# A hand-scheduled attention and FP4 feed-forward kernel: its setup, with other operands on VectorE and part of the normalisation on GpSimd

## The reference

```
xn  = (x - mean) / sqrt(var + 1e-5)
q, k, v = split(xn @ w_attn + b_attn)          # 16 heads of 8
s   = q @ k.T * 8**-0.5 + mask                 # later keys only: -log(distance + 1), earlier keys: -inf
att = softmax(s) @ v @ w_proj + b_proj
h   = silu(fq(xn) @ fq(w_gate).T) * (fq(xn) @ fq(w_up).T)       # 352 wide
ffn = fq(h) @ fq(w_down).T
fq(z): blocks of 16 along the last dimension, scale = max|z| / 6, each value rounded to the FP4 grid
```

## Time and profile before

| | before |
|---|---|
| median of three runs | 626.64 us |
| the profiled execution, its own time | 626.35 us |
| its span in the profile | 624.5 us |
| TensorE busy | 564.4 us, 90% |
| VectorE busy | 562.8 us, 90% |
| GpSimd busy | 537.4 us, 86% |
| ScalarE busy | 400.8 us, 64% |

### The profile page before, as it was taken

The page is one execution under the profiler, slowest core; times in us unless marked ns, Lnnn a source line. Parts: engine busy times, 40 slices in busy tenths (PEclk is TensorE's granted clock), DMA queues, the critical chain, the costliest instruction groups (busy, mean ns, idle before and its releaser), DMA issues.

```text
span 624.5 us, 11270 instructions
## 1 busy us (share of the span) xinstructions
PE 564.4 (90%) x3807; PEld 250.9 (40%) x3807; DVE 562.8 (90%) x1178; ACT 400.8 (64%) x857; POOL 537.4 (86%) x400
## 2 busy tenths in 40 slices
PE   6999779999999999999989899999989898989985
PEld 5576534444343334333333332342334242432322
DVE  6899998989999999999999999998989999997661
ACT  4576457566656475767667577666656667759782
POOL 7226987789899989999998999999998999998992
PEclk9999988999999999999999999999999999999997
DMA  5255341310000000200000000000000000000000
GB/s 148 74 137 114 119 83 51 78 43 36 2 2 3 0 2 10 86 1 2 2 0 2 19 1 1 2 2 1 1 2 1 19 0 2 1 2 1 1 2 17
DMA packets 14715, 16.66 MB, mean 27 GB/s; under 512 B 1594, under 2 KB 14171, under 8 KB 14243
## 3 DMA queue, kind: packets, MB, share of 16 engines
q1 hardware_dynamic: 14123, 15.70, 9.2%
q10 hardware_dynamic: 536, 0.26, 0.2%
HBM read 11.75 MB, written 4.01 MB: 25 GB/s over the span
## 4 chain that ended last, share of the span: by engine, by line
PE 43%; POOL 32%; DVE 13%; ACT 7%; issue 4%; ACTq 0%; POOLq 0%; DVEq 0%
POOL ring L802 25%; PE psum L1396 11%; PE psum L1354 9%; PE psum L1378 7%; DVE mxp L1135 7%; ACT ring L954 2%; POOL xw L820 2%; POOL xw L818 2%; PE psum L1331 2%; POOL xw L822 2%; PE psum L1312 2%; PE psum L1314 1%; PE psum L1320 1%; DVE ring L1162 1%; PE psum L1404 1%
## 5 line engine op out<-in xcount | busy, mean ns | idle before, releaser
L802 POOL TENSOR_TENSOR ring<-ring,dist 128x1024 f32<-128x1024 f32 (+3 forms) x223 | 438.4, 1996 | 31.7 <-ACT ring L954 31.3
L1135 DVE TENSOR_REDUCE mxp<-psum 128x1 f32<-128x512 f32 (+3 forms) x640 | 352.6, 598 | 20.5 <-PE psum L1354 11.4
L954 ACT ACTIVATE ring<-psum 128x512 f32<-128x512 f32 (+3 forms) x446 | 211.5, 528 | 101.5 <-PE psum L1381 51.9
L1354 PE MATMUL psum<-kop,qop 96*128 96x512 bf16 (+3 forms) x640 | 198.0, 352 | 7.3 <-DVE mxp L1135 5.3
L1378 PE MATMUL psum<-qop,kop 128*128 128x512 bf16 (+3 forms) x640 | 190.7, 349 | 6.2 <-DVE mxp L1135 3.7
L1396 PE MATMUL psum<-ring,vaug 128*32 128x512 f32 (+3 forms) x1280 | 151.5, 544 | 15.0 <-POOL ring L802 14.1
L1162 DVE TENSOR_TENSOR ring<-psum,dist 128x512 f32<-128x512 f32 (+3 forms) x194 | 115.7, 622 | 13.9 <-ACT psum L954 13.8
L954 ACT ACTIVATE psum<-psum 128x512 f32<-128x512 f32 (+3 forms) x194 | 99.5, 543 | 39.7 <-PE psum L1378 23.4
L1354 PEld LDWEIGHTS psum<-kop,qop 96*128 96x128 bf16 x640 | 57.2, 97 | 127.8 <-DVE mxp L1135 46.5
L1378 PEld LDWEIGHTS psum<-qop,kop 128*128 128x128 bf16 x640 | 59.7, 97 | 82.2 <-DVE mxp L1135 15.5
L1357 PE MATMUL psum<-tri_q,identb 128*128 128x128 bf16 x256 | 56.2, 221 | 0.0
(11 more groups left out here) (130 smaller groups left out, 490.2 us busy)
## 6 DMA issues: line engine op xcount, KB each, us to landing
kop<-parts_dram SPq DMA_DIRECT2D x9, 384.0 KB
qop<-parts_dram SPq DMA_DIRECT2D x9, 384.0 KB
parts_dram<-qpart SPq DMA_DIRECT2D x18, 128.0 KB, 2.8
xin<-_attn_hidden_states_dram SPq DMA_DIRECT2D x4, 256.0 KB, 4.7
ring<-inv_dram SPq DMA_DIRECT2D x1, 1024.0 KB, 4.9
out_dram<-xin SPq DMA_DIRECT2D x4, 256.0 KB, 2.3
parts_dram<-qpart SPq DMA_DIRECT2D x6, 96.0 KB
qop<-parts_dram SPq DMA_DIRECT2D x3, 192.0 KB
```

Of the source, the lines that this page charges most:

```text
L802: g_.tensor_tensor(slot(p)[:, :, 0:n], slot(p)[:, :, 0:n], both, ALU.mult).then_inc(weighed_pool, 1)
L954: a_.activation(scores if pair_vec[p] else slot(p)[:, e % 2, 0:n], scores, ACT.Exp, scale=SCALE).then_inc(exp_done, 1)
L1135: v_.tensor_reduce(mxp[:, u % 2, 4 * a + j, c - g:c - g + 1], bank(*o)[:, 0:n], AX_X, ALU.max).then_inc(max_used, 1)
L1354: ins = mm(bank(*o)[:, 0:n], qop[0:K_MAX, u // NQ % 2, h, P * a:P * (a + 1)], kop[0:K_MAX, h, k0:k0 + n], start=True, stop=(c != g))
```

## The change

- **Normalisation.** VectorE still normalises chunk ci = 0. For the other three it works out mean and reciprocal deviation once for all 12 tiles, and GpSimd does the two elementwise steps (subtract, multiply) for each chunk, 128x512 each, as item `scale`.
- **First split.** The remainder of the bf16 split of chunk 0 stays in the PSUM bank of `qk` instead of going to the SBUF buffer `qc`; the bank is free only after the last step of the split.
- **Quantisation.** The reciprocals of the block scales and the exponent bits are written to a PSUM bank (`c4`), which each piece holds from stage 2 to stage 5; the scales lie in rows of 35 columns, written as 5 x 7. The weights are three pieces (384, 384, 352) instead of two of 560, and come after the four of `xn`. The wait for GpSimd moves from stage 4 to stage 5. Seven pieces in all.
- **Loads.** For the second group q and k come in two parts, heads 0 to 3 first (`next_loaded`), then the rest; the loads of the FFN weights move behind them in SyncE's queue, and GpSimd's memset that they wait for moves to the end of its constants.
- **ScalarE's constants** for later chunks are written in quarters (four instructions of 1024 columns).
- **Plan.** 20 instead of 30 warming transposes; ranks of `dist` and `v` go from 4 and 3 to 8, those of `sel` for heads 1 to 3 to 4.3; the max pass of unit 0 goes head by head; `CHUNK_AT` holds back `qk` and `v` and no longer the normalisation; an idle engine now steps to the nearest clock of any other engine.

```diff
-    add("DVE", ("inv",), 700, 100, [], rank=0)
-    add("DVE", ("kfill", 0), 3300, 100, [], rank=0)
+    add("DVE", ("inv",), 2150, 100, [], rank=0)
+    add("DVE", ("kfill", 0), 1750, 100, [], rank=0)
...
-        add("DVE", ("scale", ci), 2000, 100, [("ACT", ("sqrt", 0 if ci == 0 else NG - 1))], at=at, rank=1 if ci < 2 else 3)
-        pe(("xnT", ci), 8 * P, [("DVE", ("scale", ci))], rank=1)
+        if ci < 2:
+            add("DVE", ("scale", ci), (2800, 800)[ci], 100, [("ACT", ("sqrt", NG - 1 if ci else 0))], rank=1)
+        if ci:
+            pool(("scale", ci), 2600, [("DVE", ("scale", 1))], rank=2)
+        pe(("xnT", ci), 8 * P, [("POOL" if ci else "DVE", ("scale", ci))], rank=1)
...
-            pe(("sel", t, h), PARTS * GQ, [("DVE", ("rest", t, 1)), ("POOL", ("consts",))], rank=1)
+            pe(("sel", t, h), PARTS * GQ, [("DVE", ("rest", t, 1)), ("POOL", ("consts",))], rank=SEL_RANK if h else 1)
...
+            if kind == "fp4" and item[2] == 2 and len(free_banks(now)) < HELD_FREE:
+                return None
...
+        if engine == "DVE" and kind == "scale":
+            now = max(now, clock["POOL"] if pool_busy[0] else 0)
...
-            others = [clock[e] for e in busy if clock[e] > now]
+            if engine == "POOL":
+                pool_busy[0] = False
+            others = [clock[e] for e in busy if e != engine]
...
+                if o[0] == "scale":
+                    ci = o[1]
+                    tiles = slice(TPG * CHUNKS[ci], TPG * (CHUNKS[ci] + 1))
+                    xn = xw[:, 0:S].rearrange("p (t d) -> p t d", d=D)[:, tiles]
+                    pool.wait_ge(rstd_ready, 1)
+                    g_.tensor_tensor(xn, xin[:, tiles], moments[:, tiles, 0:1].to_broadcast([P, TPG, D]),
+                                     ALU.subtract).then_inc(centred, 1)
+                    pool.wait_ge(centred, ci)
+                    g_.tensor_tensor(xn, xn, st1[:, 0, tiles].rearrange("p (t o) -> p t o", o=1).to_broadcast(
+                        [P, TPG, D]), ALU.mult).then_inc(xn_pool, 1)
...
-                    ins = v_.tensor_scalar(sc[:, of], amax[:, of], 1.0 / 6.0, 1e-12, ALU.mult, ALU.max)
+                    ins = v_.tensor_scalar(sc[:, n].rearrange("p (a b) -> p a b", b=7), amax[:, n],
+                                           1.0 / 6.0, 1e-12, ALU.mult, ALU.max)
...
-                    ins = v_.reciprocal(amax[:, of], sc[:, of])
+                    bank_free_for(vec, "c4", n)
+                    ins = v_.reciprocal(bank("c4", n)[:, 0:nb], sc[:, n, 0:nb])
...
-                    if n:
-                        vec.wait_ge(fp4_seq, 2 * n)
-                    ins = v_.tensor_scalar(c.bitcast(I32), v.bitcast(I32), EXPONENT, None, ALU.bitwise_and)
+                    ins = v_.tensor_scalar(bank("c4", n)[:, 0:w].bitcast(I32), v.bitcast(I32), EXPONENT, None,
+                                           ALU.bitwise_and)
...
-                    v_.tensor_scalar(c, c, 1.0, ROUND, ALU.max, ALU.mult).then_inc(round_ready, 1)
+                    if n:
+                        vec.wait_ge(fp4_seq, 2 * n)
+                    v_.tensor_scalar(c, bank("c4", n)[:, 0:w], 1.0, ROUND, ALU.max, ALU.mult).then_inc(round_ready, 1)
...
-                        v_.scalar_tensor_tensor(out=rest(t), in0=bank("qk", 0, t), scalar=bqk[:, t:t + 1],
+                        v_.scalar_tensor_tensor(out=bank("qk", 0, t), in0=bank("qk", 0, t), scalar=bqk[:, t:t + 1],
...
-                        v_.tensor_tensor(qpart[:, t, 2], rest(t), qpart[:, t, 1], ALU.subtract).then_inc(part3_vec, 1)
+                        v_.tensor_tensor(qpart[:, t, 2], bank("qk", 0, t), qpart[:, t, 1],
+                                         ALU.subtract).then_inc(part3_vec, 1)
```

More of the change, by code:

```diff
@@ L131, in plan @@
             act(("p2", ci, t), GQ, [("DVE", ("rest", t, 0)) if ci == 0 else ("POOL", ("split", 2 * ci + t, 0))], rank=1)
-        pe(("v", ci), 4 * GQ, [("ACT", ("xnT", ci))] + first, rank=3)
+        pe(("v", ci), 4 * GQ, [("ACT", ("xnT", ci))] + first, at=at, rank=V_RANK)
         act(("v", ci), P, [("PE", ("v", ci))], n=4, rank=3)
         if ci:
-            add("ACT", ("kfill", ci), 3500, 200, first, at=at, rank=4)
-            if ci == 1:
-                add("ACT", ("qzero", 1), 3500, 200, first, at=at, rank=4)
+            for part in range(4):
+                if ci == 1:
+                    add("ACT", ("qzero", 1, part), 920, 200, first, at=at, rank=4)
+            for part in range(4):
+                add("ACT", ("kfill", ci, part), 920, 200, first, at=at, rank=4)
     for k in range(FILL):
@@ L145, in plan @@
     for k in range(NG):
-        pe(("dist", k), 4 * GQ, [("DMA", ("hankel",)), ("POOL", ("consts",))] + first, rank=4)
+        pe(("dist", k), 4 * GQ, [("DMA", ("hankel",)), ("POOL", ("consts",))] + first, rank=DIST_RANK)
         act(("dist", k), GQ, [("PE", ("dist", k))], rank=3)
@@ L176, in plan @@
                         needs = [("DMA", ("q", u // NQ)), ("DMA", ("k", CHUNKS.index(c)))]
+                        if u == NQ:
+                            needs = [("DMA", ("next", 0))]
                     if u >= 2:
@@ L251, in plan @@
     clock = {e: 800.0 for e in queues}
-    seen = {("DMA", ("x", ci)): 4700 + 700 * ci for ci in range(NG)}
+    seen = {("DMA", ("x", ci)): 4750 + 700 * ci for ci in range(NG)}
     seen[("DMA", ("hankel",))] = 25000
-    seen[("DMA", ("weights",))] = 52000
+    seen[("DMA", ("weights",))] = WEIGHTS_AT
     pair_vec, weighed_by = {}, {}
@@ L270, in released @@
               "up": ("ACT", ("gu",) + o[1:])}.get(kind)
+        if kind == "c4":
+            by = ("DVE", ("fp4", o[1], FP4_STAGES - 1))
         if kind == "sel":
@@ L273, in released @@
         if kind == "qk":
-            by = ("DVE", ("rest", o[2], 0)) if o[1] == 0 else ("ACT", ("qf",) + o[1:])
+            by = ("DVE", ("rest", o[2], 1)) if o[1] == 0 else ("ACT", ("qf",) + o[1:])
         if kind == "st":
@@ L332, in take @@
             issued[kind] += 1
+        if engine == "DVE" and kind == "fp4" and item[2] == 2:
+            o = ("c4", item[1])
+            b = min(free_banks(now), key=lambda k: (released(holder[k]) if holder[k] else 0, k))
+            bank_of[o], prior[o], holder[b] = b, holder[b], o
         if engine == "ACT" and kind == "st":
@@ L375, in take @@
                 seen[("DMA", ("k", ci))] = end + DMA_CHUNK
+                if ci == 1:
+                    seen[("DMA", ("next", 0))] = end + DMA_NEXT
                 for gi in range(1, NG):
```

208 lines of the change are left out of this document (120 added, 88 removed).

## The result

The changed kernel took 622.65 us, the median of five runs (622.03 to 623.89), against 626.68 us for the kernel before. The ratio is 0.9929, with a 95% interval of 0.9916 to 0.9941: faster by 0.7%, 4 us, where 12 us were forecast. The direction was right, the size was a third, inside the range from 605 to 624 only at its end. The profiled execution took 622.93 us, with a span of 621.2.

A forecast was written before the change was run, and what follows sets the result against it. VectorE was taken to bound the setup, sharing the steady stage's weighing with GpSimd. Terms of 12.3 + 2.4 + 1.8 = 16.5 us of VectorE's time, worth 10.4 to 16.5, were taken as 12: 614.5 against 626.64 us, range 605 to 624.

The forecast's parts named there:

- the part on the loads: SyncE's queue: weight loads moved behind the q and k loads cost nothing, covered by the four `xn` pieces going first.
- The port: VectorE's quantisation: product L1049 saves 2.8 us, exponent steps L1054 and L1058 1.7; PSUM operands cost 2.0 and 1.1.
- L1045: VectorE's scale in the quantisation: 3.1 us saved, with no instruction over about 0.2 us afterwards.
- L1080: Last step of the first split, before the first scores: 0.68 us each with one PSUM input, 1.4 us saved.
- The normalisation: VectorE's L1022: of 6.8 us, 1.84 stay for the first chunk and 5.0 us go.
- The head of the chain: TensorE's first transposes: fewer warming ones and the repaired idle rule start the chain 2.4 us earlier, near 10.3 us.
- The square root's 1.8 us: VectorE's idle wait near 31 us for ScalarE's root goes, by later `dist` and `v` and quartered constants: 1.8 us.
- The first weighing: GpSimd's first weighing, at 60.52 us before, was to start between 50 and 57 us.
- The rate of 0.63: Steady stage, weighing shared with GpSimd: 1 us of VectorE replaces 0.63 us of time, so 16.5 us give 10.4.
- The gain is given back: Rival: GpSimd is the real bound, VectorE's freed time turns idle; 624 us or no change, chance 0.13.
- Everything shifts: Rival: setup bound by VectorE alone, steady stage starts 16.5 us earlier; 610 us, down to 605, chance 0.25.
- The ping-pong through the shared buffer: Rival: stage 5 waits for GpSimd's step of the piece before, 3.7 us for six pieces; 636 us, chance 0.09.

The follow-up runs named there:

- experiment 1: Changed kernel with the plan told that the weights land at 78 us instead of 62 (`WEIGHTS_AT`), orders replanned: 613.50 us, ratio 0.9774.
- experiment 2: Changed kernel with the eight weight loads back in their old place in SyncE's queue, all orders unchanged: 612.46 us, ratio 0.9770.
- experiment 4: Changed kernel with the weight loads early and the quantisation through SBUF instead of the PSUM bank: 619.14 us, ratio 0.9880.
- 11: Changed kernel with early weight loads and the remainder of the first split in its SBUF buffer again, orders unchanged: 613.71 us, ratio 0.9777.
- 7: Changed kernel with early weight loads and the last three chunks' normalisation back on VectorE, replanned: 611.90 us, ratio 0.9752.
- 6: Kernel before with only the new idle rule and 20 instead of 30 warming transposes: 624.91 us, ratio 0.9954.
- experiment 12: Changed kernel with early weight loads, the second group's q and k loaded whole, and the plan told when they land: 612.74 us, ratio 0.9774.
- Experiment 9: Changed kernel with early weight loads, the last three chunks' normalisation on VectorE and 100 instead of 200 fillers: 617.35 us, ratio 0.9838.
- experiment 10: Changed kernel with early weight loads and the second group's q and k loaded whole, orders unchanged: 628.22 us, ratio 1.0009.

## Why the prediction was wrong

**The step that failed** is this one of the part on the loads: "I cost the move at nothing: the cover is the four pieces of `xn` that go ahead." The cover ran out at 67.7 us, the weights landed at about 75.7. I looked at what the queue move took away from the stores and not at when the moved loads would arrive. The plan's own number for it, raised with the move from 52 to 62 us, was not checked against the queue. The queue of the kernel before:

```profile
24.37 2.20 SPq L640 DMA_DIRECT2D qop<-parts_dram  x3
...
30.12 1.31 SPq L633 DMA_DIRECT2D kop<-parts_dram  x3
...
31.94 7.17 SPq L690 DMA_DIRECT2D xw<-in_L_ffn_w_gate_dram  x1
...
40.60 1.50 SPq L692 DMA_DIRECT2D wp<-in_L_attn_w_proj_dram  x1
```

From the first of its twelve loads to the issue of the last weight load it takes 16.2 us, with one slow issue of 7.17 us among them, and that load lands 6.6 us later. Counted from 45.84 us, where the changed kernel's twelve loads start, this gives a landing at 68.7 us (an estimate). It would have shown that there was no margin, and that 62 us was wrong, but only 1 us of the wait: the changed kernel has two slow stretches in its queue, 7.07 and 7.42 us, where the kernel before has one.

The move cost a wait of 8.0 us, and 9 to 10 us of time (experiments 1 and 2). What the lower clock had in the 1 to 2 us beyond the wait was not measured by itself. The last sign that the prediction named for being wrong, that VectorE's idle time near the pieces grows, is what came. Without the wait the kernel takes 612.5 or 613.5 us, where 614.5 were forecast.

**The other steps.**
- The port, that is, what VectorE loses to GpSimd in the product and the exponent steps. In the sum, the product and the two steps of the exponent gave 4.5 us less 3.1 us for PSUM, a net of 1.4. The runs give 6.7 us for the same operands (4 against 2). The durations were right, but the stretches would have been longer in the new order: 1330 ns for the product instead of the 1012 of the earlier trace rows. The new order fills GpSimd earlier (7.42 against 0.64 us from 30 to 40 us), so that more of these steps have a GpSimd instruction beside them.
- L1045. I expected nothing over 0.2 us. Its successor L1144 took 1.04, 0.67 and 0.76 us; against the 3.1 us taken, the group's 3.6 us for seven instructions hold 3.6 - 7 x 0.18 = 2.3 us of stretch still, so that 0.8 us went. Without the wait for the weights, in experiment 2, the seven take 4.5 us, and nothing went. This term should have been near zero.
- L1080: 1.4 us was the right size for the wrong reason. The stretch is gone in SBUF too (11); the order took it away, not PSUM.
- The normalisation: 5.0 us of VectorE's time taken as gain. Given back to VectorE they are 3.25 us and cost no time (7). The term was too high by 1.75 us in its size, and no run shows that the rest reaches the end.
- The head of the chain, 2.4 us: transposes at 10.00 us instead of 10.3. The two lines alone gave 2.4 us, but with the shorter wait for the square root in it (6).
- The square root's 1.8 us: in the changed kernel VectorE has no wait of its kind left, and maxima run in its place. Its share of the time was not measured.
- The first weighing was to start between 50 and 57 us. It starts at 59.76, against 60.52 before. But GpSimd's idle time in front of it did shrink: it is busy for 39.3 of the first 60 us in experiment 2 and for 25.6 before, since the normalisation (6.2 us) and much of the quantisation and splitting moved in there. The memset of `hT`, which follows its last step of the last piece, comes 13.2 us earlier in experiment 2, the second row here, than in the kernel before:

```profile
107.90 0.31 POOL L793 MEMSET hT<- 1x256 f32 x1
```
```profile
94.71 0.31 POOL L884 MEMSET hT<- 1x256 f32 x1
```

- The rate of 0.63 can't be read from these runs. In the first 100 us the maxima take 35.8 us of VectorE before (78 instructions) and 50.3 us in experiment 2 (106), 14.5 us more, and the end comes 14.4 us earlier (0.9770 of the kernel before's 627). That looks like one to one, but it isn't a rule: in experiment 1 the maxima take 55.1 us and in experiment 12 only 43.1, and both kernels end within about 1 us of the same time.

So 614.5 without the wait was partly luck: the port's worth was put too low, and L1045 and the normalisation too high.

**The rivals.** "The gain is given back" had the number, 624, and not the mechanism: VectorE's idle time came from a DMA, not from GpSimd as the bound. Its condition that the first weighing still starts at about 60 us did hold, and cost nothing. "Everything shifts" is close to what the kernel does once the wait is gone. The ping-pong through the shared buffer did not appear; VectorE's wait for GpSimd's step is 0.2 us at most in experiment 2 and 1.7 us, once, in experiment 12.

**What stays open.** The operands (6.7 us) and the two lines of the idle rule (2.4 us) make 9 of the 14.4 us, if they add, which no run shows. Loads by heads, the split's PSUM operand and GpSimd's share of the normalisation show no worth of their own (12, 11, 7). The other 5 us are in the ranks, the quarters, and the order of the pieces, which were not taken apart. Experiment 9 shows a replanned kernel 5 us off what its parts let expect, so that small differences between replanned kernels mean little.

## What to carry to other kernels

In a kernel with a fixed order, these late transfers had no cost as long as the order's idea of their landing was true, and more than the length of the wait when it was not: a wait of 8.0 us cost 10, one of 12.4 us cost 15.8, and telling the plan the truth (62 to 78 us, 13 to 31 us) brought each back without moving a byte. Before costing a moved load at nothing, add up the issues in front of it in its queue and compare the landing with the first instruction that waits; if hardly any margin is left, count a second slow issue. Look also at what the wait counts: here it took in a transfer that the waiting instruction did not need. And a saving in front of such a wait is invisible: 6.7 us measured as some 2, so find the wait before judging the saving.

## What the runs showed of the hardware

A VectorE instruction with one f32 SBUF input of 35 elements and its output written as 5 x 7 was still held up by GpSimd. In the changed kernel it began at 35.26 us and ended, after 1.04 us, with this instruction of GpSimd:

```profile
34.99 1.26 POOL L874 TENSOR_TENSOR xw<-xw,hT 128x512 f32<-128x512 f32 x1
```

Alone it takes 0.17 us, so the odd shape did not free it from GpSimd. The Trainium skill, page "VectorE: DVE Perf Modes", section "Mode 2×_2P — use both read ports for one tensor", has the two-port mode only where the outermost non-unit dimensions of source and destination are both even or equal; 35 and 5 are neither, and read so the row differs from it. The 5 x 7 lie in one run, though; if they count as one dimension of 35, source and destination are equal and the row agrees. No run here tells the two apart. The kernel before wrote its 35 columns in one run, and there an instruction was held up in the same way, VectorE's row in front, GpSimd's behind it; the two end together:

```profile
60.00 0.59 DVE L1045 TENSOR_SCALAR sc<-amax 128x35 f32<-128x35 f32 x1
```
```profile
59.19 1.36 POOL L782 TENSOR_TENSOR xw<-xw,hT 128x560 f32<-128x560 f32 x1 [5.23 <-DVE hT L1058]
```

Issuing one transfer took SyncE's queue 7.42 us behind twelve loads of q and k (7.17 us in experiment 2, 8.02 in experiment 1), where most of its neighbours take 0.4 to 0.6. The slow stretch can be longer: in experiment 10 the three loads of k, of 384 KB each, took 14.44 us to issue, in the changed kernel three of k and the weight transfer behind them 14.5 us together.

And VectorE's exponent steps with an f32 operand in PSUM take 0.68 us for 512 columns, where the SBUF form undisturbed takes 0.43. Beside a busy GpSimd the SBUF form of the first of them took 0.93 us in the mean (experiment 4), so that the slower PSUM form won here.
